# First attention of a hybrid block: output projection over 512 query columns, softmax shares as a row, heads summed transposed, feature tables split by ScalarE and VectorE alone

## The reference, cut to what matters

```python
# x: (B=4, L=1024, D=128) float32; 8 heads, key and value width 128
x = x + attn_a(_layernorm(x), ...)          # attention with relative positions
x = x + ffn(_layernorm(x), ...)             # 8 experts, top 2
x = x + attn_b(_layernorm(x), ...)
x = x + ffn(_layernorm(x), ...)

# attn_a
Q = (q @ w_qs) * scale ; K = q @ w_ks ; V = q @ w_vs          # per head
attn = einsum('bnqd,bnkd->bnqk', Q + rel_embed_bias, K)
rel_k = positions @ w_rel_pos_k     # positions: 2L-1 rows of 192 features
attn_pos = relative_shift(einsum('bnqd,nkd->bnqk', Q + rel_pos_bias, rel_k))
a = softmax(attn + attn_pos, axis=-1)
out = einsum('bnqk,bnkd->bnqd', a, V)
return out.transpose(0, 2, 1, 3).reshape(B, L, H * Dv) @ w_out + b_out
```

## Time and profile before

| what | before |
|---|---|
| three timed executions | 2703.06, 2704.85, 2710.36 us, median 2704.85 |
| profiled execution, its time | 2695.13 us |
| its span | 2693.2 us |
| mean granted clock of TensorE, share of full speed | 0.939 |
| TensorE busy | 2459.4 us, 91% of the span, 13784 matmuls |
| TensorE weight loads | 1923.0 us, 71% |
| VectorE | 1857.6 us, 69%, 4854 instructions |
| ScalarE | 1548.6 us, 58%, 3107 |
| GpSimd | 451.5 us, 17%, 827 |
| DMA | 385.55 MB in 153098 packets, of it SyncE's queue 345.74 MB |
| chain that ended last | TensorE 76%, VectorE 11%, ScalarE 4% |

### The profile page before, as it was taken

One profiled execution on the slowest core, in us unless ns is written; L12 is line 12 of the kernel. 1 busy time (PEld: TensorE's weight loads), 2 busy tenths in 40 slices (PEclk: granted clock), 3 DMA queues, 4 the chain that ended last, 5 costly groups with the idle time before them and its releaser, 6 DMA issues.

```text
span 2693.2 us, 41229 instructions
## 1 busy us (share of the span) xinstructions
PE 2459.4 (91%) x13784; PEld 1923.0 (71%) x13784; DVE 1857.6 (69%) x4854; ACT 1548.6 (58%) x3107; POOL 451.5 (17%) x827
## 2 busy tenths in 40 slices
PE   4999899999999999999999987789999989988776
PEld 3788787788888888888888865665555545544565
DVE  4677776666777777767776654588877877873544
ACT  3666665556766666666566643537766656645333
POOL 1000012000000022000020004522222223424154
PEclk7999999999999999999999998879999989998886
DMA  3665568556665566665566536400000000000364
GB/s 122 235 216 202 181 231 283 201 189 210 212 211 206 196 208 225 209 217 196 184 231 214 206 107 184 150 22 1 1 1 1 1 7 11 21 8 14 96 194 124
DMA packets 153098, 385.55 MB, mean 143 GB/s; under 512 B 17972, under 2 KB 74932, under 8 KB 152564
## 3 DMA queue, kind: packets, MB, share of 16 engines
q1 hardware_dynamic: 137562, 345.74, 37.5%
q0 software_dynamic: 12208, 35.62, 4.3%
q10 hardware_dynamic: 3120, 1.57, 0.2%
HBM read 192.02 MB, written 193.53 MB: 143 GB/s over the span
## 4 chain that ended last, share of the span: by engine, by line
PE 76%; DVE 11%; ACT 4%; issue 3%; another core or an unknown queue 2%; DMA 2%; POOL 1%; SPq 0%; DVEq 0%; ACTq 0%; POOLq 0%
PE ps L425 8%; PE ps L427 8%; PE ps L426 8%; PE ps L996 8%; PE ps L1063 5%; PE ps L1102 5%; PE ps L971 5%; PE ps L970 5%; PE ps L1084 5%; PE ps L1009 4%; PE ps L1011 4%; PE ps L1010 4%; DVE ps L1756 1%; DVE r_mx L1760 1%
## 5 line engine op out<-in xcount | busy, mean ns | idle before, releaser
L1275 ACT ACTIVATE a_Ph<-ps 128x512 fp32r<-128x512 f32 x512 | 305.1, 596 | 471.4 <-PE ps L996 471.4
L1324 ACT ACTIVATE r_P<-ps 128x512 f32<-128x512 f32 (+3 forms) x768 | 329.9, 492 | 199.3 <-PE ps L1084 175.9
L1673 DVE CUSTOM_DVE_ANT_0 a_sp<-ps,a_sp 128x1024 f32<-128x1024 f32 x256 | 313.2, 1223 | 178.5 <-PE ps L427 160.2
L1679 DVE TENSOR_TENSOR a_Pl<-ps,a_Ph 128x512 fp32r<-128x512 f32 x512 | 349.0, 682 | 10.0 <-ACT a_Ph L1275 10.0
L970 PE MATMUL ps<-a_fa,a_ua 128*128 128x384 f32 (+2 forms) x960 | 329.2, 355 | 28.5 <-ACT a_rt L1259 14.5
L1267 ACT ACTIVATE a_sp<-a_sp,a_nm 128x1024 f32<-128x1024 f32 x256 | 294.8, 1152 | 45.7 <-DVE a_nm L1673 45.1
L996 PE MATMUL ps<-ident,a_sp 128*128 128x128 f32 x2048 | 310.2, 274 | 0.0
L1063 PE MATMUL ps<-r_K,r_Q 128*128 128x512 f32 (+3 forms) x768 | 280.8, 406 | 28.2 <-DVE r_mx L1756 14.6
L996 PEld LDWEIGHTS ps<-ident,a_sp 128*128 128x128 f32 x2048 | 252.6, 141 | 62.3 <-issue 1.2
L971 PE MATMUL ps<-a_fb,a_ub 86*128 86x384 f32 (+2 forms) x960 | 291.8, 319 | 0.0
L1756 DVE CUSTOM_DVE_ANT_0 ps<-ps,r_maskq 128x256 f32<-128x256 f32 (+3 forms) x512 | 244.5, 504 | 39.0 <-PE ps L1063 36.6
...
## 6 DMA issues: line engine op xcount, KB each, us to landing
scr<-a_rt SPq DMA_DIRECT2D x256, 576.0 KB
a_sp<-scr SPq DMA_DIRECT2D x256, 512.0 KB, 4.4
...
a_wc<-wsp SPq DMA_DIRECT2D x24, 512.0 KB, 5.5
...
wsp<-a_wc SPq DMA_DIRECT2D x8, 512.0 KB, 5.6
...
```

The source lines that it names most:

```text
L1324: e.activation(self.P[:, pt, off:512], ps[:, bank, off:512], ACT.Exp).then_inc(S["b_exp"], 1)
L1673: e.tensor_tensor_reduce(out=w, in0=ps[:, 2:4, :].rearrange("p a n -> p (a n)"), in1=w, scale=-1.0, scalar=3e38, op0=ALU.add, op1=ALU.min, ...
L1679: e.tensor_tensor(self.Pl[:, n % 3, :], ps[:, 4 + n % 2, :], self.Ph[:, n % 3, :].bitcast(F32), ALU.subtract).then_inc(S["p_lo"], 1)
```

## The change

- `out`: three matmuls of 512 columns with `wc` as weights and `osh`, `osl` as the moving side. The result has the output width on the partitions and 512 queries in the row, so heads are summed in this form, in a new tile `xT` (128 x 1024) for a batch. After the last head a new unit `xt` (twice a batch) turns four blocks of 128x128 back on TensorE, and VectorE adds them to `x`.
- The reciprocals of the sums are numbers on the partitions, but are now needed along the row. A new unit `share` (step `kq` = 0) takes them on VectorE one step earlier, and SyncE writes them to DRAM (`rdr`); unit `rows` (step `kq` = 2) waits for that and reads the 512 numbers back to all 128 partitions (`share` tiles). VectorE multiplies the product in bank 7 by them in place and adds it to `xT`. For the first head of a batch the product is written to `xT` alone.
- `Ph` and `Pl` have two buffers instead of three. The side units of the layer norms, the routing and the sending of rows stand three steps later.
- Opening: ScalarE multiplies by the mask as it copies, VectorE makes the low part, one table each time, between the halves of the first layer norm; GpSimd has no part. The second table is loaded with 96 rows instead of 86, ten of them zero. `x`, the masks and the tables are loaded from ScalarE's queue; on SyncE's, `bias` and `f0` go before the weights.

The names of the new semaphores and the wait of `first_attention_done` are left out here.

```diff
@@ -98,8 +98,8 @@
     ln = splits(0)(0, 6)
-    p = [("mix", 0), ("load", 1)] + ln[:4] + [("prod", 0, 7)] + ln[4:] + [("cut",)]
-    p += [("u", 0, 0, 2), ("u", 0, 1, 3), ("copy", 0), ("table",), ("g", 0, 4)]
+    p = [("mix", 0), ("load", 1)] + ln[:3] + [("table", 0), ln[3], ("prod", 0, 7), ln[4], ("table", 1), ln[5]]
+    p += [("u", 0, 0, 2), ("u", 0, 1, 3), ("copy", 0), ("g", 0, 4)]
@@ -121,10 +121,13 @@
         for i, it in enumerate(splits(1)(b - 1, 7) + gates(0, b - 1) + place(0, b - 1)):
-            extra.setdefault(64 * b + 6 + i, []).append(it)
+            extra.setdefault(64 * b + 9 + i, []).append(it)
+    for b in range(B):
+        for half in range(2):
+            extra.setdefault(64 * b + 67 + 4 * half, []).append(("xt", b, half, 7))
...
         for i, it in enumerate(disp(0, part) + [("m_bias", 0, c) for c in PARTS[part]]):
-            extra.setdefault(64 * b + 21 + i, []).append(it)
+            extra.setdefault(64 * b + 24 + i, []).append(it)
@@ -151,6 +154,8 @@
             p.append(("out", pq - 1, 7))
+        if kq == 2 and tlive:
+            p.append(("rows", pq))
@@ -163,6 +168,8 @@
             p += [("tlow", pq, jb), ("pv", pq, ja)]
+        if kq == 0 and tlive:
+            p.append(("share", pq))
@@ -488,6 +495,13 @@
             self.w1st, self.w1r = (c.enter_context(nc.sbuf_tensor("a_" + n, [128, 2, 512], F32)) for n in ("w1st", "w1r"))
+        self.share = []
+        for skip in (3712, 2048):
+            with ExitStack() as c:
+                c.enter_context(nc.sbuf_tensor(f"a_skip{skip}", [128, skip], F32))
+                self.share.append(c.enter_context(nc.sbuf_tensor(f"a_share{skip}", [128, 512], F32)))
@@ -512,7 +526,8 @@
             self.gah, self.gal = sb("gah", [128, 2, 512], F32R), sb("gal", [128, 2, 512], F32R)
-            self.Ph, self.Pl = sb("Ph", [128, 3, 512], F32R), sb("Pl", [128, 3, 512], F32R)
+            self.Ph, self.Pl = sb("Ph", [128, 2, 512], F32R), sb("Pl", [128, 2, 512], F32R)
+            self.xT = sb("xT", [128, L])
@@ -520,9 +535,10 @@
             self.wsp = nc.dram_tensor("wsp", (H, 128, 1024), F32, kind="Internal").ap()
+            self.rdr = nc.dram_tensor("rdr", (2, 512), F32, kind="Internal").ap()
...
             flat = lambda i: self.sp[:, i:i + 2, :].rearrange("p a n -> p (a n)")
-            self.raw = flat(0), flat(2)[0:NFB, :]
+            self.raw, self.padded = (flat(0), flat(2)[0:NFB, :]), flat(2)[0:96, :]
@@ -578,13 +594,9 @@
-        weight_loads(0)
-        e.dma_start(self.x[:, 0:8, :], xin[:, 0:8, :]).then_inc(self.d_x[0], 16)
...
         e.dma_start(self.f0[:, :], bass.AP(dr["feat0"].tensor, 0, [[0, 128], [1, 96]])).then_inc(S["d_bias"], 16)
-        e.dma_start(self.tmask[:, :], dr["tmask"]).then_inc(S["d_tmask"], 16)
-        e.dma_start(self.raw[0], dr["feat_a"]).then_inc(S["d_tab"], 16)
-        e.dma_start(self.raw[1], dr["feat_b"]).then_inc(S["d_tab"], 16)
+        weight_loads(0)
@@ -616,6 +628,18 @@
                 self.load_rows(e, u)
+            elif u[0] == "share":
+                qd = u[1]
+                e.wait_ge(S["r_inv"], qd + 1)
+                e.dma_start(self.rdr[qd % 2, :].rearrange("(p k) -> p k", k=4), self.rv[:, 4 * (qd % 2):4 * (qd % 2) + 4]).then_inc(
+                    S["d_rw"], 16)
+            elif u[0] == "rows":
+                qd = u[1]
+                e.wait_ge(S["d_rw"], 16 * (qd + 1))
+                if qd:
+                    e.wait_ge(S["x_add"], qd)
+                e.dma_start(self.share[qd >= 16][:, :], bass.AP(self.rdr.tensor, 512 * (qd % 2), [[0, 128], [1, 512]])).then_inc(
+                    S["d_rr"], 16)
@@ -691,11 +715,6 @@
                allow_small_or_imprecise_dtypes=True).then_inc(S["const"], 1)
-        e.wait_ge(S["d_tmask"], 16)
-        for k, n in enumerate((128, NFB)):
-            e.wait_ge(S["tab_hi"], k + 1)
-            e.tensor_scalar(self.raw[k], self.raw[k], self.tmask[0:n, 2 * k + 1:2 * k + 2], None, ALU.mult).then_inc(
-                S["tab_cut"], 1)
@@ -998,7 +1017,7 @@
                 _, qd, j = u
-                slot, b = (8 * qd + j) % 3, qd // 16
+                slot, b = j % 2, qd // 16
@@ -1014,12 +1033,18 @@
                 e.wait_ge(*free[bank])
+                mm3(e, ps[:, bank, :], self.wc[:, slot, 0, 384:512], self.wc[:, slot, 1, 384:512], self.osh[:, :],
+                    self.osl[:, :]).then_inc(S["out_mm"], 1)
+                free[bank] = S["x_add"], qd + 1
+            elif u[0] == "xt":
+                _, b, half, bank = u
+                e.wait_ge(S["x_add"], 16 * b + 15 + half)
+                e.wait_ge(*free[bank])
                 for k in range(4):
-                    cs = slice(128 * k, 128 * k + 128)
-                    i = mm3(e, ps[:, bank, cs], self.osh[:, cs], self.osl[:, cs], self.wc[:, slot, 0, 384:512],
-                            self.wc[:, slot, 1, 384:512])
-                i.then_inc(S["out_mm"], 1)
-                free[bank] = S["x_add"], qd + 1
+                    c0 = 512 * half + 128 * k
+                    i = e.transpose(ps[:, bank, 128 * k:128 * k + 128], self.xT[:, c0:c0 + 128], ident[:, :])
+                i.then_inc(S["xt_mm"], 1)
+                free[bank] = S["x_fin"], 2 * b + half + 1
@@ -1212,7 +1237,11 @@
         S, ps = self.S, self.ps
-        xin = self.dr["q"].rearrange("(n p) d -> p n d", p=128)
+        dr, xin = self.dr, self.dr["q"].rearrange("(n p) d -> p n d", p=128)
+        e.dma_start(self.x[:, 0:8, :], xin[:, 0:8, :]).then_inc(self.d_x[0], 16)
+        e.dma_start(self.tmask[:, :], dr["tmask"]).then_inc(S["d_tmask"], 16)
+        e.dma_start(self.raw[0], dr["feat_a"]).then_inc(S["d_tab"], 16)
+        e.dma_start(self.padded, dr["feat_b"]).then_inc(S["d_tab"], 16)
@@ -1231,10 +1260,12 @@
-            elif u[0] == "cut":
+            elif u[0] == "table":
+                k, n = u[1], (128, NFB)[u[1]]
+                e.wait_ge(S["d_tmask"], 16)
                 e.wait_ge(S["d_tab"], 32)
-                for k in range(2):
-                    e.activation(self.cut[k], self.raw[k], ACT.Copy).then_inc(S["tab_hi"], 1)
+                e.activation(self.cut[k], self.raw[k], ACT.Copy, scale=self.tmask[0:n, 2 * k:2 * k + 1]).then_inc(S["tab_hi"], 1)
@@ -1263,16 +1294,15 @@
-                    e.wait_ge(S["x_add"], t // 4 - 3)
+                    e.wait_ge(S["r_inv"], t // 4 - 3)
...
                 e.wait_ge(S["t_mm"], n + 1)
-                if n >= 3 and u[2] >= 2:
-                    e.wait_ge(S["pv_mm"], n - 2)
-                e.activation(self.Ph[:, n % 3, :], ps[:, 4 + n % 2, :], ACT.Copy).then_inc(S["p_hi"], 1)
+                if n >= 2:
+                    e.wait_ge(S["pv_mm"], n - 1)
+                e.activation(self.Ph[:, n % 2, :], ps[:, 4 + n % 2, :], ACT.Copy).then_inc(S["p_hi"], 1)
@@ -1629,11 +1659,10 @@
             elif u[0] == "table":
-                for k, n in enumerate((128, NFB)):
-                    e.wait_ge(S["tab_cut"], k + 1)
-                    e.scalar_tensor_tensor((self.fa, self.fb)[k][:, :], self.cut[k].bitcast(F32),
-                                           self.tmask[0:n, 2 * k:2 * k + 1], self.raw[k], ALU.mult,
-                                           ALU.add).then_inc(S["tab_lo"], 1)
+                k, n = u[1], (128, NFB)[u[1]]
+                e.wait_ge(S["tab_hi"], k + 1)
+                e.scalar_tensor_tensor((self.fa, self.fb)[k][:, :], self.raw[k], self.tmask[0:n, 2 * k + 1:2 * k + 2],
+                                       self.cut[k].bitcast(F32), ALU.mult, ALU.add).then_inc(S["tab_lo"], 1)
@@ -1676,24 +1705,39 @@
                 e.wait_ge(S["p_hi"], n + 1)
-                e.tensor_tensor(self.Pl[:, n % 3, :], ps[:, 4 + n % 2, :], self.Ph[:, n % 3, :].bitcast(F32),
+                e.tensor_tensor(self.Pl[:, n % 2, :], ps[:, 4 + n % 2, :], self.Ph[:, n % 2, :].bitcast(F32),
                                 ALU.subtract).then_inc(S["p_lo"], 1)
+            elif u[0] == "share":
+                qd = u[1]
+                c4 = 4 * qd % 16
+                if qd >= 2:
+                    e.wait_ge(S["d_rw"], 16 * (qd - 1))
+                e.wait_ge(S["p_exp"], 4 * qd + 4)
+                e.reciprocal(self.rv[:, 4 * (qd % 2):4 * (qd % 2) + 4], self.ls[:, c4:c4 + 4]).then_inc(S["r_inv"], 1)
...
                 _, qd, bank = u
-                c4 = 4 * qd % 16
-                if qd % 16 == 0:
-                    e.wait_ge(S["x_bias"], qd // 16 + 1)
-                if qd:
-                    e.wait_ge(S["x_add"], qd)
-                e.wait_ge(S["p_exp"], 4 * qd + 4)
-                self.step(e.reciprocal(self.rv[:, 0:4], self.ls[:, c4:c4 + 4]))
-                e.wait_ge(S["dve_step"], self.steps)
+                to, first = self.xT[:, 512 * (qd % 2):512 * (qd % 2) + 512], qd % 16 < 2
+                if qd >= 16 and first:
+                    e.wait_ge(S["xt_mm"], 2 * (qd // 16 - 1) + qd % 2 + 1)
+                e.wait_ge(S["d_rr"], 16 * (qd + 1))
                 e.wait_ge(S["out_mm"], qd + 1)
```

(23 more changed lines are left out.)

12 lines of the change are left out of this document (6 added, 6 removed).

## The result

The changed kernel takes 2678.89 us (median of 5 runs, 2673.23 to 2685.58), the kernel before beside it 2705.86 us (2703.06 to 2710.36): a ratio of 0.9897, 95% interval 0.9877 to 0.9917. The forecast was 2664, the range 2650 to 2686. The profiled execution took 2673.23 us (span 2671.5) for 2695.13 before, so 21.9 us went where 41.1 had been forecast (27.0 between the two medians). The time is right within its range; three terms of the sum are not, and the experiments are about those.

A forecast was written before the change was run, and what follows sets the result against it. TensorE was taken to bound the first attention. Projection -37.8, turns back +4.7, end +2.0 and opening -10.0 sum to -41.1 us: 2654.0 for the profiled execution, 2664 on the timed runs' scale, range 2650 to 2686.

The forecast's parts named there:

- What bounds the kernel: First attention: TensorE busy 1061 of 1070 us, so a microsecond taken from it is a microsecond of the span, unless something is uncovered.
- Output projection: TensorE, once per group of 512 queries: three matmuls for twelve, 0.70 for 1.29 us, saving 0.59 us times 64, 37.8 us.
- Turn back: Four 128x128 transposes per half batch on TensorE, 0.67 us each time; seven inside the full stretch cost 4.7 us.
- VectorE: Multiply and addition of 0.69 us each replace four additions of 1.13 us: +0.35 us a group, 22 us, none reaching TensorE.
- rival (2): VectorE late in the step: doubled multiply, 35 us, reaching TensorE whole gives 2699 us, half of it 2681; chance 0.15.
- Opening: Before the first `r` matmul: earlier tables and split start `r` at 30.3 to 31 us for 40.62; gain 10 us.
- rival (1): Opening gains 1 us for 10, the table late as before or weights pushed back by the other queue: 2673 us; chance 0.15.
- End: End of the first attention: the eighth turn back runs in single file before the next stage, costing 2.0 us (1 to 3).
- DRAM round trip: Shares written and read back on SyncE's queue: cost 0, with 10.4 us of room; TensorE feels it from about 16 us.
- two buffers: Two `Ph`/`Pl` buffers for three: cost 0, as ScalarE's wait for the transposes already implies the wait for the product.

The follow-up runs named there:

- e12_load_later: e9_split's cuts, dispatch copies paced in pieces and attention output copied in share order, on e3_behind, plus SyncE's weight loads two steps later: 2630.94 us, ratio 0.9749.
- e2_side: Changed kernel with the second layer norm, routing and dispatch back at their old steps, second turn back at step 64b+70: 2679.16 us, ratio 0.9918 to the kernel before.
- e9_split: On top of e3_behind, VectorE's two longest side units (head's weight mix, routing's slot unit) cut in two: 2634.45 us, ratio 0.9961 to the kernel before.
- e6_no_multiply: Changed kernel without the VectorE multiply by the shares, heads summed undivided: 2617.14 us, ratio 0.9882 to the kernel before.
- e1_row: Changed kernel with shares written to DRAM in query order by 4-byte writes, so the multiply reads them side by side: 2933.58 us, ratio 1.0842 to the kernel before.
- e3_behind: Changed kernel with ScalarE issuing the two feature tables only after the first head's weights have landed: 2670.32 us, ratio 0.9886 to the kernel before.

## Why the prediction was right or wrong

- **What bounds the kernel:** right for the quiet groups, too simple for the others. The list of waits showed 13 places; I read it as 15.9 us that stay as they are. It should have been read as 13 steps in which TensorE does not set the pace, and in which a saving ahead of the wait buys nothing. This is the step that failed: -37.8 was 64 times 0.59; the quiet groups gave 14.3 for 13.4, the busy ones 6.5 for 19.7. In steps 0 to 64 the runs show it (groups 16 and 24, and e12_load_later). Another 3.3 us are group 68 and belong to the copies. What is missing in groups 136 to 176, 7.4 us (6.5 in e2_side), lies round the routing's units and is explained in part only: e9_split gets 2.7 us back in steps 140 to 152, e6_no_multiply 4.6 in all, so VectorE's whole work counts there too, and no run took away the waits round step 169.
- **Output projection, 0.59 us:** right where nothing else is late (0.62 to 0.64 by the groups).
- **Turn back, 0.67 each:** the group with the turn at step 131 (22.65 before, 22.57 after, others 22.02) gives 0.55; close.
- **VectorE:** the sum of 0.69 for the multiply was too low (1.08; upper bound 1.25). The Trainium skill ("SBUF — State Buffer", the cacheline note of "Door 1: The DMA port swizzle"), which I had set against the change, was right on the direction, and e1_row shows it on one and the same instruction, 1083 to 697 ns. The end point for TensorE, zero, was nearer than rival (2)'s 35 or 17 us: without any multiply the busy groups are 7.5 us shorter in one execution, 1.4 of them by waits.
- **Opening:** mechanism right, size half: 4.7 for 10. The tables landed at 11.4 and 14.3 us (13 to 14 forecast) and the chain from the layer norm's root to `r` took 14.5 us (14.9 forecast). What failed is the start of it: I let the weights land as before or earlier and named their delay only in rival (1); the last of them landed 10.5 us after its issue for 2.0. With them ahead (e3_behind) `r` comes at 31.65.
- **End:** 3.2 for 2.1: multiply 1.05 for 0.69, and the lower clock behind TensorE's 2.03 us of standing, which I hadn't counted. My own sum also slipped: 1596.0 + 0.67 + 0.62 + 0.60 is 1597.9, not 1597.65.
- **DRAM round trip, two buffers:** right, nothing. The margin was smaller than I said: SyncE comes to `rows` 5.2 us after the write (median) and not 10.4, so a wait there begins sooner, and with 11.6 us from write to reading back the kernel lost 4 us a group (e1_row), where I had let TensorE feel it from about 16 us on.

The sum again with what was measured: -4.4 - 14.3 - 6.5 + 3.2 = -22.0, for 21.9. It came into the range because the range held rivals (1) and (2). Of (1) the mechanism is real, the weights pushed back by the other queue, at half its price; that of (2), the doubled multiply, is not what the runs show. That the sum of all this stayed inside the range is in part luck.

Open: why the clock falls after one wait of 1.40 us and not after another in the same place; how much of the loss in groups 136 to 176 is one long unit's and how much VectorE's whole work; and the last 1.3 of the 13.2 us.
